# Attention block: projections kept whole and split later, head 1 one matmul behind head 0, one exponential a head

## The reference, cut to what matters

```python
def _attn(x, ctx, Wq, Wk, Wv, Wo, bo):
    q = (x @ Wq).reshape(b, n, HEADS, DHEAD)
    k = (ctx @ Wk).reshape(b, m, HEADS, DHEAD)
    v = (ctx @ Wv).reshape(b, m, HEADS, DHEAD)
    sim = jnp.einsum('bihd,bjhd->bhij', q, k) * scale
    attn = jax.nn.softmax(sim, axis=-1)
    out = jnp.einsum('bhij,bjhd->bihd', attn, v).reshape(b, n, INNER)
    return out @ Wo + bo
h = _ln(x, g1, be1)
x = _attn(h, h, Wq1, Wk1, Wv1, Wo1, bo1) + x      # self-attention: what the change touches
```

## Time and profile before

| what | value |
|---|---|
| median of three executions | 1986.89 us |
| the profiled execution's own time | 1987.43 us |
| its span, first to last instruction | 1985.6 us |
| granted TensorE clock | full in all 40 slices |
| TensorE, VectorE, ScalarE, GpSimd busy | 99%, 70%, 58%, 75% of the span |
| GpSimd in the chunks' slices | 9 tenths in most |
| exponentials (L1289) | 512 of 1027 ns |
| adds of probabilities (L1545 and L1542) | 448 of 2391 and 2390 ns |
| row maxima (L914) | 457 of about 1220 ns |

### The profile page before, as it was taken

How to read it: one execution, slowest core, us unless ns; L and a number is a source line. 1 busy time by engine, 2 the same in 40 slices (tenths; PEclk the granted TensorE clock), 3 DMA queues, 4 the chain that set the end, 5 groups by cost and what they waited for, 6 DMA issues and landing times.

```text
span 1985.6 us, 32165 instructions
## 1 busy us (share of the span) xinstructions
PE 1973.7 (99%) x12056; PEld 1353.4 (68%) x12056; DVE 1396.3 (70%) x2437; ACT 1143.7 (58%) x2042; POOL 1490.1 (75%) x800
## 2 busy tenths in 40 slices
PE   9999999999999999999999999999999999999999
PEld 7655655666565656755655666565569999888888
DVE  6688687666868886587787666867867888744443
ACT  6665576555656666465666555656756766533332
POOL 3699899989999998899899899989996665200000
PEclk9999999999999999999999999999999999999999
DMA  7201000001000000010000001000030420000000
GB/s 256 107 28 43 6 6 17 6 27 49 17 12 6 17 6 27 8 58 6 6 22 6 27 1 54 7 27 1 23 106 22 150 65 1 1 22 33 33 11 32
DMA packets 48956, 67.15 MB, mean 34 GB/s; under 512 B 6177, under 2 KB 42145, under 8 KB 46753
## 3 DMA queue, kind: packets, MB, share of 16 engines
q1 hardware_dynamic: 48800, 65.10, 10.2%
HBM read 45.17 MB, written 19.92 MB: 33 GB/s over the span
## 4 chain that ended last, share of the span: by engine, by line
PE 94%; POOL 3%; DVE 2%; issue 1%; ACT 1%; POOLq 0%; DVEq 0%
PE score L576 22%; PE score L555 19%; PE score L702 9%; PE attn_project L511 8%; PE attn_project L687 5%; PE attn_project L716 5%; PE score L523 5%; PE score L657 4%; PE score L625 3%; PE first_score L537 3%; PE attn_project L537 3%; PE score L561 3%; POOL acc L1545 2%; PE first_score L671 1%; PE first_score L587 1%
## 5 line engine op out<-in xcount | busy, mean ns | idle before, releaser
L1545 POOL TENSOR_TENSOR acc<-acc,pT 128x1024 f32<-128x1024 f32 x384 | 918.1, 2391 | 54.7 <-POOL acc L1545 1.4
L1289 ACT ACTIVATE pT<-score 128x1024 f32<-128x1024 f32 x512 | 507.7, 1027 | 107.5 <-PE score L561 70.4
L555 PE MATMUL score<-qk 64*128 64x512 f32 x3072 | 466.5, 405 | 0.9 <-ACT pT L1289 0.4
L576 PE MATMUL score<-pT,vT 128*64 128x512 f32 x1952 | 432.3, 595 | 0.0
L555 PEld LDWEIGHTS score<-qk 64*128 64x128 f32 x3072 | 269.0, 184 | 123.3 <-ACT pT L1289 82.0
L914 DVE TENSOR_REDUCE nmax<-attn_project 128x2 f32<-128x1024 f32 x256 | 312.7, 1221 | 7.3 <-PE attn_project L537 3.9
L576 PEld LDWEIGHTS score<-pT,vT 128*64 128x64 f32 x1952 | 134.8, 137 | 265.8 <-issue 243.8
L914 DVE TENSOR_REDUCE nmax<-first_score 128x2 f32<-128x1024 f32 x201 | 245.1, 1219 | 0.2 <-issue 0.2
L511 PE MATMUL attn_project<-hT,wqk 128*128 128x512 f32 x738 | 185.9, 400 | 0.0
L702 PE MATMUL score<-hT,wp 128*128 128x512 f32 x768 | 183.7, 395 | 0.0
L1542 POOL TENSOR_TENSOR acc<-pT 128x1024 f32<-128x1024 f32 x64 | 153.0, 2390 | 27.5 <-ACT pT L1289 27.5
(11 more groups left out here) (202 smaller groups left out, 3127.5 us busy)
## 6 DMA issues: line engine op xcount, KB each, us to landing
xres<-x_middle SPq DMA_DIRECT2D x10, 512.0 KB, 3.6
raw_qk<-in_L_xattn_Wq SPq DMA_DIRECT2D x32, 128.0 KB, 2.2
raw_qk<-in_L_xattn_Wk SPq DMA_DIRECT2D x32, 128.0 KB, 2.4
raw_v<-in_L_xattn_Wv SPq DMA_DIRECT2D x8, 512.0 KB, 4.7
keys_all<-keys SPq DMA_DIRECT2D x1, 4096.0 KB, 13.1
values_all<-values SPq DMA_DIRECT2D x1, 4096.0 KB, 13.3
out_x<-xres SPq DMA_DIRECT2D x7, 512.0 KB, 2.9
xres<-in_x SPq DMA_DIRECT2D x3, 1024.0 KB, 5.7
```

Of the source, the lines that this page charges most:

```text
L555: last = e.matmul(bank, key_part(P, h, r, jt), queries1[P % 2][r, w, c * BANK:(c + 1) * BANK], start=(fresh and part == 0), stop=(not fres ...
L576: last = e.matmul(banks[bank][head * DH:(head + 1) * DH, :], vT[:, v_slot(D, jt), c0:c0 + DH], pT[:, jt, head, :], start=(jt == 0), stop=( ...
L1289: e.activation(pT[:, jt].rearrange("p h n -> p (h n)"), SC[R % 2][:, :], ACT.Exp).then_inc(s.exponential, 1)
L1545: e.tensor_tensor(total, total, pT[:, jt], ALU.add).then_inc(s.probs_added, 1)
```

## The change

The diff does four things. ScalarE keeps each projection whole, in float32, in SBUF (`keep_qk`): keys go to keys_whole, queries, scaled, to queries_whole, which lie where the rests will lie; the bank is free after that (qk_kept). The split of the projections of slot C - 1 then takes place in chunk C: on VectorE `change_keys` right behind `turn_max` and ahead of `fold_sums`, and `split_qk` ahead of the slot's own work; on ScalarE `split_qk` between `make_shift` and `write_oT`. On TensorE head 1's matmuls go one place behind head 0's, and a `first_score` of head 1 goes into the next round. Each head has its own exponential of 128x512. `early_max` and `row_max_of` are gone: all row maxima are of both heads.

```diff
+        queries_whole = [tile[:, N:2 * N] for tile in (qk0_whole, qk1_whole)]
+        keys_whole = [tile[:, 2 * N:3 * N].rearrange("p (c n) -> p c n", c=CHUNKS) for tile in (qk0_whole, qk1_whole)]
@@ TensorE
-                free[bank] = ((s.split_lo, qk_of[P, u]),)
+                free[bank] = ((s.qk_kept, qk_of[P, u]),)
-                need.wait_ge(s.keys_rounded, keys_of[P, half])
+                need.wait_ge(s.qk_kept, qk_of[P, half])
-                    free[f"S{R % 2}" + "ab"[head]] = ((s.exponential, R + 1),)
+                    free[f"S{R % 2}" + "ab"[head]] = ((s.exponential, 2 * R + head + 1),)
             for C in range(NC):
-                if C + 1 < NC:
-                    for head in range(2):
-                        first_score(*next_part(C + 1, 0), head)
                 for jt in range(TILES):
-                    for part in range(len(TERMS) + (jt % TPC < 2)):
-                        for head in range(2):
-                            score(TILES * C + jt, part, head)
-                    if C + 1 < NC and jt:
-                        for head in range(2):
-                            first_score(*next_part(C + 1, jt), head)
+                    parts = len(TERMS) + (jt % TPC < 2)
+                    for part in range(parts):
+                        score(TILES * C + jt, part, 0)
+                        if part:
+                            score(TILES * C + jt, part - 1, 1)
+                        elif jt and C + 1 < NC:
+                            first_score(*next_part(C + 1, jt - 1), 1)
+                    if C + 1 < NC:
+                        first_score(*next_part(C + 1, jt), 0)
+                    score(TILES * C + jt, parts - 1, 1)
+                if C + 1 < NC:
+                    first_score(*next_part(C + 1, TILES - 1), 1)
@@ VectorE
+            def change_keys(P, u):
+                whole = keys_whole[P % 2][:, u, :]
+                need.wait_ge(s.qk_kept, qk_of[P, u])
+                e.tensor_tensor(whole[:, PAIR:], whole[:, PAIR:], whole[:, 0:PAIR], ALU.subtract
+                                ).then_inc(s.keys_changed, 1)
+                need.wait_ge(s.keys_changed, keys_of[P, u])
+                e.tensor_tensor(keys_lo[P % 2][:, u, 0:PAIR], whole[:, 0:PAIR],
                                 keys_hi[P % 2][:, u, PAIR:2 * PAIR].bitcast(F32), ALU.subtract)
+            def split_qk(P, u):
                 need.wait_ge(s.split_hi, qk_of[P, u])
+                e.tensor_tensor(lo, whole, hi.bitcast(F32), ALU.subtract).then_inc(s.split_lo, 1)
                     gather_max(C + 1)
                     turn_max(C + 1)
+                for unit in units(C - 1)[0:1] if C else ():
+                    change_keys(*unit)
...
                 if C:
                     fold_sums(C - 1)
...
+                for unit in units(C - 1) if C else ():
+                    split_qk(*unit)
...
-                whole_array(slot(C), C + 2 if early_max(C + 2) else None)
+                whole_array(slot(C))
@@ ScalarE
+            def keep_qk(P, u, bank="PJ"):
+                if u < 2:
+                    e.copy(keys_whole[P % 2][:, u, :], banks[bank])
+                    e.copy(keys_hi[P % 2][:, u, PAIR:], banks[bank]).then_inc(s.qk_kept, 1)
+                else:
+                    e.activation(queries_whole[P % 2][:, (u - 2) * BANK:(u - 1) * BANK], banks[bank], ACT.Copy, scale=SCALE
+                                 ).then_inc(s.qk_kept, 1)
-            def exponential(R):
+            def exponential(R, head):
-                e.activation(pT[:, jt].rearrange("p h n -> p (h n)"), SC[R % 2][:, :], ACT.Exp
-                             ).then_inc(s.exponential, 1)
+                e.activation(pT[:, jt, head, :], banks[f"S{R % 2}" + "ab"[head]], ACT.Exp).then_inc(s.exponential, 1)
```

More of the change, by code:

```diff
@@ L897, in split_queries @@
-            def split_queries(P, u, bank):
-                span = slice((u - 2) * BANK, (u - 1) * BANK)
-                need.wait_ge(s.split_hi, qk_of[P, u])
-                hi, lo = (queries1[P % 2][:, w, span] for w in range(2))
-                e.scalar_tensor_tensor(lo, banks[bank], SCALE, hi.bitcast(F32), ALU.mult, ALU.subtract
-                                       ).then_inc(s.split_lo, 1)
-            def split_qk(P, u, bank="PJ", coming=None):
                 if u < 2:
-                    change_keys(P, u, bank, coming)
-                else:
-                    split_queries(P, u, bank)
+                    need.wait_ge(s.keys_changed, keys_of[P, u])
@@ L910, in row_max @@
+                    whole, lo = (part[P % 2][:, u, PAIR:] for part in (keys_whole, keys_lo))
+                    hi = keys_hi[P % 2][:, u, 0:PAIR]
+                else:
+                    span = slice((u - 2) * BANK, (u - 1) * BANK)
+                    whole, (hi, lo) = queries_whole[P % 2][:, span], (queries1[P % 2][:, w, span] for w in range(2))
+                e.tensor_tensor(lo, whole, hi.bitcast(F32), ALU.subtract).then_inc(s.split_lo, 1)
             def row_max(C, t, half):
@@ L1072, in _ @@
             turn_norm((1, 1))
-            for u, bank in zip((0, 2, 1), CTX_BANKS):
-                split_qk(0, u, bank)
+            for u in range(CHUNKS):
+                change_keys(0, u)
             for i in range(TILES):
@@ L1078, in _ @@
             turn_max(0)
-            split_qk(0, 3, "PJ")
-            split_qk(1, 0, "S1a")
-            split_qk(1, 2, "S1b")
+            for u in (0, 2, 1, 3):
+                split_qk(0, u)
+            change_keys(1, 0)
+            split_qk(1, 0)
+            split_qk(1, 2)
             for C in range(NC):
@@ L1257, in fold_values @@
                            banks[bank].rearrange("p (o n) -> p o n", o=2)).then_inc(s.values2_a, 1)
-            def split_qk(P, u, bank="PJ"):
+            def keep_qk(P, u, bank="PJ"):
                 need.wait_ge(s.qk_projected, qk_of[P, u])
@@ L1422, in _ @@
             for u, bank in zip((0, 2, 1), CTX_BANKS):
-                split_qk(0, u, bank)
+                keep_qk(0, u, bank)
+            for u in (0, 2, 1):
+                split_qk(0, u)
             for n in range(PAIRS // 2 * (B // 2)):
@@ L1437, in _ @@
                 for jt in range(TILES):
-                    exponential(TILES * C + jt)
+                    for head in range(2):
+                        exponential(TILES * C + jt, head)
                 if n == BC - 7 and b + 1 < B:
```

80 lines of the change are left out of this document (30 added, 50 removed).

## The result

The changed kernel takes 2145.74 us (median of four runs, 2143.55 to 2148.42) where the kernel before took 1986.86 beside it (four runs, 1986.7 to 1987.51): a ratio of 1.080, 95% interval 1.0781 to 1.0818, or 159 us more. I had forecast 2085, 98 more. The profiled execution took 2143.97 (span 2142.2), 156.5 over that of before.

What follows compares the result with a forecast made beforehand. TensorE, with no idle time, was taken to bound the kernel; the change would make column sums wait for VectorE's fold. 61 chunks at 1.6 us (0.1 stage, 1.5 late) added 98 to 1987.4: 2085 us, 8-in-10 range 1990 to 2140.

Steps and rivals of the forecast that it cites:

- The score stage: TensorE's score matmuls in a chunk: from 9.33 to 9.43 us, +0.1 a chunk, with row maxima the next limit.
- rival 3: Separate exponentials start 0.6 us apart and set the score stage at 9.63, no collision: 2005 us; chance 0.06.
- Rival 1: Subtractions fit between GpSimd's adds and maxima are no limit; score stage 8.75 us, total 1953 us; chance 0.09.
- The collision: VectorE's moved subtractions each wait for the end of a GpSimd instruction, taking 1 to 3 us instead of 0.42 and 0.69.
- Rival 2: No collision, VectorE's row maxima set the pace: +0.1 us a chunk, 1993 us; chance 0.07.
- One sign of the prediction: In the changed trace, GpSimd's adds beside the moved subtractions would be 0.2 to 0.4 us longer.
- b = 13.4: Time in a chunk when the GpSimd add that VectorE's first moved subtraction waits for ends; range 12.9 to 15.4 us.
- T = 21.0: Length of a chunk in us as set by VectorE's queue of waits, once GpSimd is no longer late.
- There are 61 chunks with such a split ... I count all alike. 61 x 1.6 = 98: Total loss over all chunks with a moved split, 1.6 us each (0.1 and 1.5 late): 98 us.
- T >= b + 7.6: Lower bound on chunk length, as the next chunk's row maxima wait for VectorE's late subtractions and inversions: 20.5 to 23.0 us.
- that range (16.9 to 19.4): When VectorE's fold of the sums ends in a chunk, in us; TensorE wants it at 16.45.
- With both in SBUF: Condition for a VectorE subtraction to collide with GpSimd's adds: both inputs in SBUF; 1.08 to 2.88 us in seven of eight cases.

Runs made afterwards that it cites:

- e3: The changed kernel with GpSimd adding 8 columns of each pT tile instead of 512: 1994.1 us, ratio 1.0036.
- e7: The kernel before, its score order and slot split kept, with head 1 one matmul behind head 0 and one exponential a head: 1995.91 us, ratio 1.0044.
- e1: The kernel before with only the new score order, an exponential for each head and whole row maxima; split stays in the slot: 2002.71 us, ratio 1.008.
- e10: The changed kernel with VectorE's split_qk behind the slot's own work instead of ahead of it: 2144.47 us, ratio 1.0793.
- f3: The changed kernel with only split_qk's VectorE subtractions replaced by a product with a constant, one SBUF input: 2109.59 us, ratio 1.0616.
- e9: The changed kernel with split_wo1 behind the fold instead of ahead of it in chunks 1 to 4: 2128.55 us, ratio 1.0707.
- e6: The changed kernel with twelve identity matmuls ahead of the column sum in the 15 chunks with long waits there: 2132.59 us, ratio 1.0745.
- f1: The kernel of e9 with identity matmuls at the column sum in 12 chunks and at head 1's first score behind layer-norm slots: 2116.71 us, ratio 1.0651.
- f2: The changed kernel with all four moved VectorE subtractions replaced by a product with a constant, one SBUF input: 2091.06 us, ratio 1.0518.
- e2: The changed kernel with the old order of scores and one exponential a round, the late split kept: 2170.32 us, ratio 1.0926.
- e12: The kernel before with two extra VectorE subtractions of 4 columns, both inputs in SBUF, behind each chunk's transposes: 1988.75 us, ratio 1.001.
- e8: The kernel of e7 with the last first_score pair behind the second value product and the fold ahead of the last maximum: 2004.35 us, ratio 1.0087.

## Why the prediction was off: the right mechanism, priced for the plain chunk

**The score stage, right.** Forecast 9.43, measured 9.40 where the maxima aren't late (e3, e7, and 26 chunks of the changed kernel; 9.7 in most of the others). The exponential of 128x512 takes 0.602 (forecast 0.59), and back to back they start 0.47 to 0.50 apart (forecast 0.49), not 0.6, so rival 3 falls. Rival 1 falls by e1 and e7: the maxima are the next limit in both orders.

**The collision, right, and the cause of nearly all.** Nearly every subtraction ends just behind the end of a GpSimd instruction, one for each: medians of 2474 and 1422 ns, and e3 with short adds brings the change from +159 to +10. VectorE's waits for a result of GpSimd come to 0.3 us in the chunks, so it isn't GpSimd's results that are late. Rival 2, with a price of 1993, is what that leaves (1994.1, with adds of 8 columns). One sign of the prediction failed: GpSimd's adds are not 0.2 to 0.4 longer (median 2.37, before 2.39); only its scaling is (1.74 for 1.29).

**The plain chunk, right.** I had b = 13.4 and the fold's end at b + 4.03 = 17.43; measured 17.45. I had T = 21.0; measured 20.7 and 21.1. Over the 36 plain chunks the growth is 1.25 each, 0.3 in the stage and 0.96 at the sum, where I took 0.1 and 1.5: the total is nearer than its parts, and that is luck.

**The failed step is "There are 61 chunks with such a split ... I count all alike. 61 x 1.6 = 98".** The column sum's part of it, 1.5 x 61 = 92, happens to match the 92 of the account, but by two errors that cancel: 0.96 in the plain chunks, 2.2 in the others. The other part, 0.1 x 61 = 6 for the stage, is 42, and the slot, 0, is 25. In place of that term the runs show:

1. *Chunks where VectorE has other work, and chunks where GpSimd has.* In the seven chunks about a layer norm with stages of 11.8 to 16.0 (13, 14, 30, 45, 46, 61, 62), hT stands behind `split_qk`'s two waits, or the maxima do: 29 us more in the stage. I had listed T >= b + 7.6 for plain VectorE work, and not added the slot's own. e10 shows that a different place only moves the wait, f3 that a shorter late pair gives back 30 us of the stage. In the eleven chunks where GpSimd is late b falls at its late end: the value products and the wait for the sum take 2.2 to 2.7 more than before, instead of 1.0, and the sum starts 18.6 to 19.5 into the chunk. I had reckoned that range (16.9 to 19.4) and then put all chunks at its early part, because GpSimd's phase in the plain chunk was the one that I worked out; its splits of value weights, 3.4 us in every eighth chunk, are in no term of the sum.
2. *A third subtraction in chunks 1 to 4.* `split_wo1` stands ahead of the fold, and the earlier trace rows had its 1.08 to 2.16 us; I used the row as evidence of the collision and did not put it in the queue with the two new ones. The sum comes at 20.3: 24 us in four chunks, 14.5 of them gone in e9 (17 in the whole kernel).
3. *The clock.* My waits were priced at their own length. But behind most waits of 2.2 to 3.8 us TensorE runs at 1.2 GHz for some us: 85 us in all, worth 20 to 25 (e6, f1, slot column). The kernel before never waited that long and showed none of it, so its rows couldn't price it; the bound should have had a term for it all the same.

Points 1 to 3 overlap, since long waits are where the clock falls: the account's rows carry both. Of the 61 us that I missed, the 26 chunks hold 115 - 26 x 1.6 = 73, and the plain ones give 36 x 0.35 = 13 back.

**What the prediction had wrong in its wording.** "With both in SBUF" is too narrow a condition (f2). And the halves don't simply add: that the stagger hides some of the lateness of the split (25 us, e2) was in neither sum.

**What stays open.** Whether the second condition is a mode of the engine or its read rate. That GpSimd's phase makes the eleven chunks dear is read from the timelines, where VectorE is ready as early as in plain chunks; no run shifted GpSimd alone, and that its splits of value weights are what delays it is argued from their place. Why the plain stage is 9.7 in alternate chunks follows from the maxima's start at 2.14 in the timeline, but no run moved only that.

## What to carry to other kernels

Before moving VectorE work out of PSUM into SBUF, look at what GpSimd does in that stretch: beside long GpSimd instructions such an operation cost the rest of a GpSimd instruction, even with 4 columns, and with 256 columns a second one behind it cost a whole instruction more. Price a new wait in every kind of chunk, not in the plainest: put each instruction of that engine's queue behind it, and ask where in the phase of the other engine it falls; the few chunks with other work on VectorE or GpSimd held most of this loss. Where the forecast puts waits of 2 us or more on TensorE, look whether the granted clock falls behind them (here it cost about a quarter of a us for each us at the lower level); idle matmuls put into the wait are the cheap test.

## What the runs showed of the hardware

- A VectorE operation of 4 columns, SBUF to SBUF, waits up to 2.3 us for GpSimd's current instruction, and its successor slips into the gap of two GpSimd instructions at 0.15 (e12).
- Subtractions of 256 columns take 0.56 where GpSimd's instruction beside them is one of 0.65, and 2.48 beside adds of 2.37 (changed kernel, chunks 33 and 9).
- A product with a constant, SBUF to SBUF, 256 columns in 0.295 us when free, waits for GpSimd as a subtraction of two SBUF tiles does: median 2.47 (f2).
- The granted clock fell to 0.50 behind most waits of TensorE of 2.2 to 3.8 us, and twelve projections took 5.40 instead of 3.02. Identity matmuls in the wait kept it up in most of those chunks (e6: 85 to 37.5 us, f1: 61 to 10).
- A pair of 64-row matmuls amid 128-row ones costs 0.58 instead of 0.23 (e8).
